# Turns of row maxima, of expert counts and of output groups placed later in a written-out order of a Mamba, attention and expert layer

## The reference

```python
x = x + ssm(layernorm(x))                 # conv, gated state-space mixer, chunks of 128
x = x + xattn(layernorm(x), ctx, ctx)     # 32 query heads, 8 key/value heads of 16
x = x + ffn(layernorm(x))                 # top 2 of 8 experts, gelu(gate) * up, down
```

```python
scores = einsum('bkgsd,bktd->bkgst', qh, kh) / sqrt(16)     # per sequence, 256 x 256 per head
attn = softmax(scores)
out = einsum('bkgst,bktd->bkgsd', attn, vh)
```

## Time and profile before

| what | us |
|---|---|
| median of 3 runs (lowest, highest) | 1454.18 (1453.34, 1455.5) |
| the profiled execution, its own time | 1459.7 |
| span of its trace | 1457.9 |
| PE busy | 1343.5 (92%) |
| DVE busy | 877.1 (60%) |
| ACT busy | 723.6 (50%) |

### The profile page before, as it was taken

The page is one execution under the profiler, slowest core; times in us unless marked ns, Lnnn a source line. Parts: engine busy times, 40 slices in busy tenths (PEclk is TensorE's granted clock), DMA queues, the critical chain, the costliest instruction groups (busy, mean ns, idle before and its releaser), DMA issues.

```text
span 1457.9 us, 23107 instructions
## 1 busy us (share of the span) xinstructions
PE 1343.5 (92%) x7729; PEld 734.2 (50%) x7729; DVE 877.1 (60%) x1838; ACT 723.6 (50%) x1390; POOL 586.2 (40%) x871
## 2 busy tenths in 40 slices
PE   6699999999999999998888888888999999999997
PEld 4456566666666665654333433323444444444443
DVE  5797898979797979757888888855111111111111
ACT  2676667667666676663576776762111111111110
POOL 1365465555455465675223245243222222222221
PEclk9899999999999999997898997988999999999999
DMA  9000000000000000000211110002443354244322
GB/s 338 10 8 5 8 5 1 12 1 12 1 8 5 8 6 8 13 1 5 97 34 34 34 34 31 30 30 74 121 134 114 66 138 135 46 130 132 58 44 29
DMA packets 40291, 73.00 MB, mean 50 GB/s; under 512 B 18544, under 2 KB 22896, under 8 KB 39152
## 3 DMA queue, kind: packets, MB, share of 16 engines
q1 hardware_dynamic: 30240, 48.10, 9.5%
q0 software_dynamic: 8736, 20.61, 7.6%
q10 hardware_dynamic: 1200, 2.82, 0.5%
HBM read 148.91 MB, written 19.99 MB: 116 GB/s over the span
## 4 chain that ended last, share of the span: by engine, by line
PE 68%; DVE 21%; issue 5%; ACT 3%; POOL 2%; DMA 1%; SPq 1%; POOLq 0%; DVEq 0%; ACTq 0%
PE work_ps L539 12%; PE gate_ps L1530 9%; PE up_ps L1530 9%; PE down_ps L1514 9%; PE work_ps L611 7%; DVE conv L820 7%; PE work_ps L544 4%; DVE maxes L1220 3%; PE work_ps L633 3%; PE work_ps L1046 3%; PE mturn_ps L544 2%; PE decay_ps L1037 2%; DVE mix L736 2%; PE decay_ps L621 2%; PE work_ps L1022 1%
## 5 line engine op out<-in xcount | busy, mean ns | idle before, releaser
L539 PE MATMUL work_ps<-xnT,w_in 128*128 128x256 f32 (+1 forms) x1216 | 299.8, 391 | 2.8 <-DVE xdt L860 2.1
L736 POOL TENSOR_TENSOR mix<-decay,cbm 128x512 f32<-128x512 f32 x128 | 182.9, 1431 | 221.6 <-ACT decay L731 190.6
L539 PEld LDWEIGHTS work_ps<-xnT,w_in 128*128 128x128 f32 (+1 forms) x1216 | 219.2, 188 | 65.1 <-issue 33.4
L727 ACT ACTIVATE decay<-decay_ps 128x512 f32<-128x512 f32 x256 | 154.3, 603 | 111.6 <-PE decay_ps L621 111.0
L1618 POOL DMA_INDIRECT out_dram<-y_out,ids x39 | 61.9, 1587 | 334.3 <-DVE row_w L1582 228.9
L1220 DVE TENSOR_REDUCE maxes<-work_ps 128x2 f32<-128x512 f32 x256 | 166.6, 683 | 33.7 <-PE work_ps L1022 32.1
L820 DVE SCALAR_TENSOR_TENSOR conv<-raw,conv_w,conv 128x256 f32<-128x256 f32 x240 | 177.7, 746 | 6.6 <-ACT conv L687 0.7
L1118 ACT ACTIVATE prob<-decay_ps 128x512 f32<-128x512 f32 x256 | 142.2, 609 | 75.3 <-PE decay_ps L1037 74.4
L1597 DVE TENSOR_TENSOR act<-gelu,up_ps 128x512 f32<-128x512 f32 x39 | 26.8, 688 | 252.1 <-PE up_ps L1530 252.1
L731 ACT ACTIVATE decay<-decay 128x512 f32<-128x512 f32 x256 | 163.9, 640 | 4.7 <-PE work_ps L539 3.0
L1530 PE MATMUL gate_ps<-w_e,xgT 128*128 x312 | 140.5, 593 | 1.4 <-ACT xgT L1547 1.0
(11 more groups left out here) (270 smaller groups left out, 1975.8 us busy)
## 6 DMA issues: line engine op xcount, KB each, us to landing
w_e<-c_experts_dram SPq DMA_DIRECT2D x39, 3072.0 KB
normed_tokens<-r_xn SPq DMA_DIRECT2D x17, 256.0 KB, 2.1
out_dram<-x_sb SPq DMA_DIRECT2D x17, 256.0 KB, 2.5
x_sb<-x_dram SPq DMA_DIRECT2D x1, 3072.0 KB, 16.8
w_in<-c_w_inT_dram ACTq DMA_DIRECT2D x1, 2560.0 KB, 12.7
w_in<-c_w_inT_dram SPq DMA_DIRECT2D x1, 2048.0 KB, 9.1
w_out<-c_w_outT_dram SPq DMA_DIRECT2D x1, 2048.0 KB, 21.9
RT<-cum_scratch SPq DMA_DIRECT2D x32, 48.0 KB
```

The lines of the kernel that those rows point to most:

```text
L539: m = e.matmul(ps[0:width, at:at + L], w_in[:, k, col:col + width], xnT[b % 2][:, k, :], start=(k == 0), stop=(k == KD - 1))
L727: e.activation(decay[s % 5][:, :], decay_ps[s % 3][:, :], ACT.Relu, scale=-1.0).then_inc(piece_done[stage], 1)
L736: return e.tensor_tensor(four(mix[s % 5]), four(decay[s % 5]), cb, ALU.mult)
```

## The change

Only numbers in `attention_slots()` change, and with them the order in which every engine meets the pieces.

```diff
-            put(n * (b - 1) + n // 2 * (h + 1) - LEAD + 2, ("n_turn", b, h))
-            put(n * (b - 1) + n // 2 * (h + 1) - LEAD + 3, ("n_copy", b, h), ("n_out", b, h))
+            put(n * (b - 1) + n // 2 * (h + 1) - LEAD + 5, ("n_turn", b, h))
+            put(n * (b - 1) + n // 2 * (h + 1) - LEAD + 6, ("n_copy", b, h), ("n_out", b, h))
...
-            put(at + 6, ("pv_turn", b, g))
+            put(at + 7, ("pv_turn", b, g))
...
-        put(at + 3, ("c_rank", g), ("c_count", g))
-        put(at + 5, ("c_logit", g), ("c_exp", g))
-        put(at + 6, ("c_slots", g))
+        apart = 4 if g < 2 else 0
+        put(at + 3, ("c_rank", g))
+        put(at + 3 + apart, ("c_count", g))
+        put(at + 5 + apart, ("c_logit", g), ("c_exp", g))
+        put(at + 6 + apart, ("c_slots", g))
         if g < 2:
-            put(at + 9, ("c_weight", g), ("c_weight_out", g))
+            put(at + 9 + apart, ("c_weight", g), ("c_weight_out", g))
     for t in range(12):
         for c in range(2):
-            put(n * 5 + 4 * t if t < 8 else n * 7 + 8 + 4 * (t - 8) + 2 * c, ("place", c, t))
+            put(n * 5 + 4 * t if t < 8 else n * 7 + 12 + 3 * (t - 8) + 2 * c, ("place", c, t))
```

## The result

The changed kernel took 1468.09 us in the median (1465.80 to 1471.51, 4 runs), beside 1454.10 us for the kernel before (1453.34 to 1455.50, 4 runs): 1.0097 of before, 95% interval [1.0076, 1.0119]. The forecast was 1442.2 us in a range of 1431 to 1452. The change made the kernel slower by 14.0 us, so the forecast is wrong in its sign. The profiled execution took 1465.8 us, span 1464.0.

A forecast was written before the change was run, and what follows sets the result against it. In the attention, DVE-limited and PE-limited stretches alternate, and PE's waits before the latter were the prize. Terms -7.2 - 3 - 3 - 0.5 + 1.7 = -12.0 us, from the 1454.2 median to 1442.2 us, range 1431 to 1452.

The forecast's parts named there:

- n_turn, "6 x 1.2 = 7.2 us": Six PE waits for nmax in sequences 2 to 7: product pulled ahead gains 7.2 us, bounds 0 and 12.
- 5 us of room of DVE: Attention's PE-limited windows: DVE has about 5 us of room in each, so it can follow an earlier PE.
- Clock, "I take a fifth, 3 us": Five PE-limited windows: fewer, shorter waits return some of 15 us lost at half speed; 3 us, bounds 0 and 15.
- pv_turn, 3 us in the last sequence: Turn behind product shortens ScalarE's dry spells, 0.6 to 0.7 us in each of five groups: 3 us, bounds 0 and 5.
- c_count, 0.5 us: Group 0's 3.46 us wait goes, but DVE is the limit around it: gain 0.5 us, bounds 0 and 3.5.
- PE will stop for a bank instead: At c_count: c_rank's six DVE operations stay in one piece, so PE stops about one or two pairs later.
- costs the same: c_logit, c_slots and c_weight move with c_count and cost the same as before.
- POOL has room (4 to 7 us of 18 or 20): Packing place into three slots a tile on POOL costs 0, bound 1 us, because POOL has room.
- DVE at pv_out, 1.7 us: Turn only one slot ahead of pv_out: DVE waits 0.1 us in 17 places, cost 1.7 us, bounds 0 and 26.
- the sign of a wrong forecast: Prediction wrong if DVE's waits at pv_out reach 10 us, or attention's length is unchanged with those waits gone.
- The rival that ended at 1466 us: Slower: DVE, having caught up, loses 1.0 us at pv_out in each of 26 groups; 1466 us, chance 7%.
- the waits move: Rival: PE's stop goes from nmax to the next fold's bank and DVE gives no time back; 1448 us, 20%.

The follow-up runs named there:

- e16_pv_counts: The whole change without n_turn's part (pv_turn and the counts moved, n_turn where it was), against the kernel before: 0.9998 [0.9975, 1.0020].
- e2_pvturn: Only pv_turn moved, one slot later and behind the product, against the kernel before: 1.0009 [0.9984, 1.0033].
- e17_pv_counts_logit_kept: pv_turn and the counts moved, but n_turn, c_logit and c_exp where they stood, against the kernel before: 0.9994 [0.9966, 1.0021].
- e3_counts: Only the counts' part moved (c_count, c_logit, c_slots, c_weight and the packed late places), against the kernel before: 1.0034 [1.0014, 1.0053].
- e15_counts_again: The counts' part whole, once more, beside a new set of runs of the kernel before: 1.0015 [0.9996, 1.0034].

## Why the prediction was wrong

*n_turn, "6 x 1.2 = 7.2 us".* This step failed. The wait for `nmax` went, the product was pulled ahead (780.35 us, in front of the stop; in `e16_pv_counts` 783.99, behind it), and I had foreseen the remaining stop at `pv_turn`. But I ended the count at the product and did not ask what PE meets next. The next piece, `r_turn`, hangs on the same `r_stats`: POOL's Newton steps, then ScalarE's row. In the changed kernel it starts 787.50 - 780.44 = 7.06 us behind `r_stats`, and 7.05 to 7.06 in each of the first four sequences. In `e16_pv_counts`, with the product behind the stop, it is 7.06 us as well in this sequence:

```profile
783.47 0.27 PE L1030 MATMUL work_ps<-ident,nmax 128*16 128x128 f16 x2 [2.23 <-DVE nmax L1229]
...
783.99 1.06 PE L1048 MATMUL work_ps<-prob,v_aug 128*32 128x512 f32 x8
```

```profile
788.12 0.63 PE L546 MATMUL work_ps<-ident,r_xn 128*128 128x128 f32 x4 [0.96 <-ACT r_xn L1139]
```

```profile
781.06 1.27 DVE L1259 BATCH_NORM_STATS2 r_bn<-x_sb 128x6 f32<-128x512 f32 x2
```

There the product only filled time in which PE would have waited for the row; in the other five sequences of that trace `r_turn` came 7.52 to 8.63 us behind. In the kernel before `r_turn` came 7.07 to 8.93 us behind `r_stats`; what lies above 7.06 adds up to 3.9 us over the first six, and by this reading of one trace that was the most that an earlier PE could gain here, not 7.2. "5 us of room of DVE" was the wrong test, since the limit is a chain through DVE, POOL and ScalarE, none of which is full. Measured alone, the part is +0.43%, 6.3 us the other way.

*Clock, "I take a fifth, 3 us", bounds 0 and 15.* This step failed in its sign, and it is the loss: some 32 us more at half clock, some 16 us of PE work, against 7.7 us less idle time. I took it that fewer stops could only help. The stops were moved and in part shortened, not removed, and where they now stand the dense stretch behind them runs partly at half clock in each of five sequences, for some 20 us in all (10 in the trace of before). Filling the stops with useless matmuls takes 1.0097 to 1.0015, and `n_turn` alone from 1.0043 to 1.0005. Added work can give back time only if the idle time cost more than its own length, and the stretches behind the filled stops are the ones back at full clock: the first pair shows by this that the clock is the cause. In which stretches the 14 us lie is less sure, as the traces of before and after differ most late, where the filler left 14.1 us for slots 208 to 216. The Trainium skill (TensorE: Matmul & The Clock Gate, "A second HAM failure mode: psum-queue depth-cycling") has short idle spells between groups of matmuls, frequent enough, swing the clock; the filler runs agree. The same page's "HAM oscillation", which ties the fall to long waits, would leave this change without a cost: the stop ahead of the slow stretch is 1.95 us, and the one stop above 3 us, at the `max` behind the count, was there before with 3.46. I had weighed the two only for a gain.

*pv_turn, 3 us in the last sequence.* The undisturbed groups behave as worked out: from one turn to the next 960.71 - 955.34 = 5.37 us, for 5.9 before and 5.2 expected. Alone the part measures 1.0009, so the gain of 3 us is not found; half a microsecond for each of a few groups is below what the runs can tell.

```profile
955.34 0.66 PE L546 MATMUL work_ps<-ident,pv 128*128 128x128 f32 x4
...
960.71 0.66 PE L546 MATMUL work_ps<-ident,pv 128*128 128x128 f32 x4
```

*c_count, 0.5 us.* Its 3.46 us wait of the earlier trace rows has become one of 3.69 us at a `max`, as the prediction foresaw ("PE will stop for a bank instead"), and nothing is gained (group 0 alone 1.0004). `c_logit` "costs the same": not refuted. "POOL has room (4 to 7 us of 18 or 20)" gives what POOL was busy in four windows, not its room, and leaves out 898 to 918 us with 13.53 of 20; nothing hung on it.

```profile
877.88 0.23 PE L1074 MATMUL work_ps<-chosen,m_ones 128*128 128x64 bf16 x1
```

*DVE at pv_out, 1.7 us.* Mis-sized as a wait; the cost is too small to be tested. The waits grew by 11.4 us, over the 10 us that I named as the sign of a wrong forecast, but `pv_turn` alone has 22.8 us of them and is not shown to cost anything (1.0009 [0.9984, 1.0033]). The rival that ended at 1466 us for this reason named nearly the right time for the wrong reason. Of the rivals none had the clock fall further; "the waits move" had the first half of what happened.

*Left open.* Which stop makes the clock fall. `e2_pvturn` has stops for `nmax` up to 3.5 us, 19.7 us in all, and is not shown to lose; the changed kernel has mostly shorter ones and loses 1%. Why `n_turn`'s share is 0.4% alone and 0.85 to 1% beside the counts, with `pv_turn` or without, is open too. The filler changed several stops at once, so it tells that they matter together, not which. And whether the counts cost a few tenths of a percent or nothing can't be told.

## What to carry to other kernels

When a wait is taken away, follow the waiting engine to the next thing that it needs, and ask whether that hangs on the same releaser: if it does, the gain is what the engine was late there, not the wait. For a PE close to full, a moved stop is priced by the clock of the dense stretch behind it, with a bound on the loss side as large as that on the gain side. A profile is one execution, and here the clock fell in other places from one to the next, so a difference between two traces needs others beside it. A filler of matmuls that writes the same bank again is a cheap test of whether idle PE time costs its own length or the clock as well.

## What the hardware showed that was not expected

More work made the changed kernel faster: 20 extra matmuls in each of six sequences, 1.0097 to 1.0015 of before.

The small DVE operation L1303 took 1.29 us and L1305 0.97 us beside POOL's addition at 962.46 us, and 0.19 us each in `e17_pv_counts_logit_kept`, where no addition ran; the reduction L1304 between them took 0.18 and 0.19 us. The Trainium skill (SBUF — State Buffer, "SBUF: two separate sides") says that DVE and GpSimd hold a pair of ports by turns, a whole instruction long, and that a DVE operation with two inputs in SBUF needs it; these rows agree, since L1303 and L1305 have two inputs and L1304 has one.

Executions of one and the same kernel differ by which dense stretches fall to half clock. `e3_counts` and `e15_counts_again` are one kernel: slots 48 to 56 took 11.1 us in the profile of the first and 12.7 in that of the second, slots 144 to 152 took 12.4 and 10.7.
